# A four-layer network on one core: a band scratch with the heads innermost, a third thread for the last attention's maxima, and gates computed first

## The reference, cut to what matters

```
L0 attn  banded: 16 heads, each token looks at the 32 tokens up to itself;
         out = einsum('bntd,bntde->bnte', softmax(bond - 10 * damage), val_win)
L0 ffn   8 low-rank experts, gated per sequence
L1 attn  causal, 8 local heads over 512 tokens, 8 global heads over 128 compressed ones
L1 ffn   8 experts, 128 -> 512 -> 128, gate = softmax of the top 2
L2 attn  linear: q, k = relu(.) + eps; kv = k'v; z = 1 / (q . sum(k) + eps)
L2 ffn   16 experts of width 64, top 4 gates, and one shared expert
L3 attn  16 heads of width 8: softmax(q k' * scale) v, divided by
         denom = mean over batches and tokens of the norm of each head's output
L3 ffn   64 experts of width 64, sigmoid gates, best 4 of 8 groups, top 8, and one shared
```

## Time and profile before

| | us |
|---|---|
| median of three runs (lowest, highest) | 3850.13 (3846.57, 3855.36) |
| the profiled execution | 3852.74 |
| its span, first to last instruction | 3851.0 |
| mean granted TensorE clock | 0.878 of full speed |
| DMA traffic | 355.91 MB, 331910 packets, 98529 of them under 512 B |

### The profile page before, as it was taken

The page is one execution under the profiler, slowest core; times in us unless marked ns, Lnnn a source line. Parts: engine busy times, 40 slices in busy tenths (PEclk is TensorE's granted clock), DMA queues, the critical chain, the costliest instruction groups (busy, mean ns, idle before and its releaser), DMA issues.

```text
span 3851.0 us, 43741 instructions
## 1 busy us (share of the span) xinstructions
PE 3115.1 (81%) x16174; PEld 1567.3 (41%) x16174; DVE 2426.6 (63%) x4576; ACT 1662.7 (43%) x2458; POOL 596.6 (15%) x425
## 2 busy tenths in 40 slices
PE   3647868997699868997699968998699977996698
PEld 1124423553245433554245532554235532464145
DVE  4634876568756776568765776668755786634442
ACT  3504625465255634465154644446154643432231
POOL 2001000311023010321013010321013110211030
PEclk8568969998799979998699989998799988997696
DMA  3151175302842165402843047412753128412261
GB/s 112 27 95 58 46 123 139 113 14 77 145 144 68 28 106 154 124 22 60 152 133 88 20 104 121 151 39 50 136 133 102 32 81 136 137 58 65 57 203 45
DMA packets 331910, 355.91 MB, mean 92 GB/s; under 512 B 98529, under 2 KB 264225, under 8 KB 330081
## 3 DMA queue, kind: packets, MB, share of 16 engines
q1 hardware_dynamic: 331697, 353.11, 39.1%
HBM read 302.74 MB, written 49.66 MB: 92 GB/s over the span
## 4 chain that ended last, share of the span: by engine, by line
PE 52%; DVE 28%; DMA 7%; ACT 5%; issue 4%; POOL 2%; SPq 2%; ACTq 0%; DVEq 0%; POOLq 0%
DVE MX L1596 7%; PE PS L1805 6%; PE PS L1828 6%; PE PS L1832 5%; PE PS L1659 5%; PE PS L1667 5%; PE PS L1103 3%; DVE U L891 3%; PE PS L1773 3%; DVE U L898 3%; DMA UU<-k_scratch 3%; PE PS L1784 2%; DVE D L1650 2%; POOL D L1404 1%; DVE D L948 1%
## 5 line engine op out<-in xcount | busy, mean ns | idle before, releaser
L1404 POOL TENSOR_TENSOR D<-D,GW 128x512 f32<-128x512 f32 x320 | 434.7, 1359 | 1409.1 <-ACT D L1477 1173.6
L783 ACT ACTIVATE U<-U 128x2048 f32<-128x2048 f32 x256 | 488.0, 1909 | 184.3 <-DVE U L891 99.4
L1645 DVE SCALAR_TENSOR_TENSOR D<-D,PS 128x512 f32<-128x512 f32 x336 | 229.2, 682 | 399.2 <-ACT D L1481 283.6
L1477 ACT ACTIVATE D<-PS 128x512 f32<-128x512 f32 x336 | 200.2, 596 | 610.2 <-PE PS L1828 610.2
L1805 PEld LDWEIGHTS PS<-WST,D 128*128 128x128 f32 (+1 forms) x2688 | 353.0, 198 | 163.4 <-DVE D L1650 96.0
L1805 PE MATMUL PS<-WST,D 128*128 128x128 f32 (+1 forms) x2688 | 380.3, 286 | 29.3 <-DVE D L1650 29.2
L1832 PE MATMUL PS<-XT,WST 128*128 128x512 f32 (+1 forms) x672 | 372.6, 637 | 29.2 <-DVE D L1645 28.0
L898 DVE SCALAR_TENSOR_TENSOR U<-PP,RD,QB 128x512 f32<-128x512 f32 x512 | 364.1, 780 | 47.5 <-ACT QB L780 28.8
L1103 PE MATMUL PS<-U,resident 128*32 128x512 f32 x2048 | 304.6, 675 | 102.3 <-ACT U L783 102.3
L1828 PE MATMUL PS<-XT,WST 128*128 128x512 f32 (+1 forms) x672 | 369.6, 633 | 7.7 <-DMA WST<-in_pairs_dram 4.7
L1596 DVE TENSOR_REDUCE MX<-PS 128x2 f32<-128x1024 f32 x256 | 298.4, 1221 | 84.9 <-PE PS L1751 84.9
(11 more groups left out here) (345 smaller groups left out, 3907.2 us busy)
## 6 DMA issues: line engine op xcount, KB each, us to landing
GW<-gates_scratch SPq DMA_DIRECT2D x320, 256.0 KB, 4.3
WST<-in_pairs_dram SPq DMA_DIRECT2D x336, 192.0 KB, 2.4
U<-band_scratch SPq DMA_DIRECT2D x32, 1280.0 KB, 14.6
UU<-in_w_dram SPq DMA_DIRECT2D x64, 512.0 KB, 7.6
UU<-pad_scratch SPq DMA_DIRECT2D x8, 1792.0 KB
UU<-q_scratch SPq DMA_DIRECT2D x24, 384.0 KB
UU<-k_scratch SPq DMA_DIRECT2D x24, 384.0 KB
e_scratch<-D SPq DMA_DIRECT2D x8, 1024.0 KB, 4.5
```

Source lines behind the costliest of these rows:

```text
L783: e.activation(ring(i), ring(i), ACT.Gelu).then_inc(S["act"], 1)
L1404: e.tensor_tensor(AV[:, n % 3, :], AV[:, n % 3, :], GW[:, p // 2 % GWS, p % 2, :], ALU.mult).then_inc(S["gated"], 1)
```

## The change

1. **Band scratch.** Its shape becomes (4, 128, 160, 16): the head is the innermost index. A row's weights go out as one run of 32 x 16 numbers (2 KB) in place of 16 runs of 32 (128 B), and come back as one run of 160 x 16 numbers (10 KB) in place of 16 runs of 160 (640 B). TensorE's moving operand at L1154 (L1167 after) is then read with 64 bytes between its elements. Zeroing the scratch at the start has the same runs.
2. **Third thread c** (turn 1): the split of q and k, their way out and back, the scores and maxima and the way of the negated maxima into the stack. It is woven among the layer-3 pairs. The scores are now 64 steps of one matmul in PZ(2), each after the maximum of the one before; a maximum covers one bank, not two. s2 stands behind the pairs, with the two sums of the exponentials (`sel_den`) as steps of its own, 66 steps in all, and their reciprocals and the norm work behind it. The sum of squares of a sequence (`norm_sum`, `norm_copy`, `norm_store`) goes to the next sequence's f1, and for the last sequence to the end of its thread.
3. **Gates first.** Layer 2's gate matmul and top 4 come before the linear attention, layer 3's gates directly behind the gate matmul, and its pairs directly behind them.
4. **Buffers.** RC and N3 lie in the gate tiles; the expert weights of f1 lie in GW (experts 0 to 3) and UU (4 to 7), where they were all in UU; the first matmul of a sequence's f1 waits for the last exponential of the sequence before.
5. **Final loads.** `sp_before_final` stands behind the last pair loads (it stood before them), and loads six sequences in place of seven; the seventh is loaded behind s2's scores.

The core of the diff; a_ lines first, the table STARTS (and TURN = 428.30, now 415.20) left out:

```diff
-        z_dram = nc.dram_tensor("band_scratch", (NT, NH, P, BAND), FP32).ap()
+        z_dram = nc.dram_tensor("band_scratch", (NT, P, BAND, NH), FP32).ap()
-                dst = bass.AP(z_dram.tensor, j * NH * P * BAND, [[BAND + 1, P], [P * BAND, NH], [1, HOR]])
+                dst = bass.AP(z_dram.tensor, j * NH * P * BAND, [[(BAND + 1) * NH, P], [1, HOR * NH]])
-                e.dma_start(band(j), z_dram[j].rearrange("n p t -> p n t")).then_inc(S[f"band{j}"], 16)
+                e.dma_start(band(j), z_dram[j]).then_inc(S[f"band{j}"], 16)
-                                            band(j)[:, 8 * h + 2 * q + r, 0:w], start=(j == 0 and r == 0),
+                                            band(j)[:, 0:w, 8 * h + 2 * q + r], start=(j == 0 and r == 0),
...
+        RC = G4[:, :, :, :].rearrange("p (h k) j n -> p h (k j n)", h=2)
+        w1slot = lambda x: (GWF, UU)[x // 4][:, 2 * FF * (x % 4):...]
...
+        def c_dve(e, b):
+            e.wait_ge(S["qk3"], at("qk3", b, 2))
+            yield from dve_split(e, F3[:, :, :], lambda k: SPL3[:, :, k, :], "split3")
+            for k in range(64):
+                yield
+                e.wait_ge(S["s1_3"], at("s1_3", b, k + 1))
+                e.tensor_reduce(MX3[:, k % NT:k % NT + 1, k // NT], PSall[:, 6:7, :], AX.X, ALU.max)...
+        def c_pe(e, b):
+            for k in range(64):
+                yield
+                if k == 0:
+                    e.wait_ge(S["stacked3"], ...); e.wait_ge(S["padded3"], ...); e.wait_ge(S["qk3"], ...)
+                else:
+                    e.wait_ge(S["max3"], at("max3", b, k))
+                e.matmul(PZ(2), QS3[:, hd, P * j:P * j + P], KS3[:, hd, :], start=True, stop=True)...
...
             yield from b_pe_pairs(e, b, 3)        # b_pe: now before s2
+            for x, k in enumerate(B_STEPS):       # s2, 64 scores and two sums
+                if x == 0:
                     e.wait_ge(S["nm_in3"], at("nm_in3", b, 48))
+                    e.wait_ge(S["sl"], at("sl", b, 2 * PAIRS))
+                    e.wait_ge(S["uv"], at("uv", b, PAIRS))
+                    e.wait_ge(S["b_f"], at("b_f", b, 3))
+                if k is None:
+                    e.matmul(PZ(x % 3), cn("sel_den"), OS3[:, h, :], start=True, stop=True)...
...
                             if b > 0:             # b_pe, first matmul of f1
-                                e.wait_ge(S["b_f"], at("b_f", b - 1, 3))
+                                e.wait_ge(S["p3"], at("p3", b - 1, STEPS3))
...
+            if b == B - 1:                        # b_sp, behind the pair loads
+                sp_before_final(e)
+                if x == 4:
+                    e.wait_ge(S["s2_3"], at("s2_3", b, STEPS3 - 1))
+                    if b == B - 1:
+                        final_load(e, B - 2, "fin_in7")
...
-            weave(thread(a_sp, e, 0), thread(b_sp, e, 1))
+            weave(thread(a_sp, e, 0), thread(b_sp, e, 1), thread(c_sp, e, 1))
```

More of the change, by code:

```diff
@@ L1701, in b_pe @@
             w2 = cn("qkv2")
+            for j in range(NT):
+                last = e.matmul(PZ(0)[:, 2 * P + E2 * j:2 * P + E2 * j + E2], XT(b)[:, P * j:P * j + P], cn("gates")[:, 8:8 + E2], start=(j == 0), stop=False, skip_group_check=True)
+            last.then_inc(S["gate_ps"], 1)
             e.matmul(PZ(1), w2[:, 0:C], XT(b), start=True, stop=True).then_inc(S["l2_ps"], 1)
@@ L1717, in b_pe @@
             yield
+            e.wait_ge(S["gate_dve"], at("gate_dve", b, 3))
+            for j in range(NT):
+                last = e.transpose(PZ(0)[0:E2, P * j:P * j + P], GT[:, j, 0:E2], ident)
+            last.then_inc(S["gate_ps"], 1)
+            yield
             e.wait_ge(S["l2_dve"], at("l2_dve", b, 4))
@@ L1731, in b_pe @@
             w3 = cn("wqkv3")
+            for j in range(NT):
+                last = e.matmul(PZ(0)[:, E3 * j:E3 * j + E3], XT(b)[:, P * j:P * j + P], cn("gates")[:, 24:88], start=(j == 0), stop=(j == NT - 1), skip_group_check=True)
+            last.then_inc(S["gate_ps"], 1)
             for k in range(2):
@@ L1758, in b_pe @@
             last.then_inc(S["gate_ps"], 1)
-            yield
-            e.wait_ge(S["nm3"], at("nm3", b, 1))
-            for j in range(NT):
-                last = e.transpose(PZB(1)[0:48, P * j:P * j + P], NM3[:, j, :], identb[:, :])
-            last.then_inc(S["nm_t3"], 1)
+            yield from b_pe_pairs(e, b, 3)
             def weighted(s):
@@ L1860, in sp_before_final @@
                 e.wait_ge(S[s], at(s, B - 1, 0))
-            for k in range(B - 1):
+            for k in range(B - 2):
                 final_load(e, k, "fin_in")
@@ L1945, in _ @@
             ready(e)
-            weave(thread(a_act, e, 0), thread(b_act, e, 1))
+            weave(thread(a_act, e, 0), thread(b_act, e, 1), thread(c_act, e, 1))
             act_final(e)
@@ L1952, in _ @@
             ready(e)
-            weave(thread(a_dve, e, 0), thread(b_dve, e, 1))
+            weave(thread(a_dve, e, 0), thread(b_dve, e, 1), thread(c_dve, e, 1))
             dve_final(e)
@@ L1959, in _ @@
             ready(e)
-            weave(thread(a_pe, e, 0), thread(b_pe, e, 1))
+            weave(thread(a_pe, e, 0), thread(b_pe, e, 1), thread(c_pe, e, 1))
             pe_final(e)
```

375 lines of the change are left out of this document (202 added, 173 removed), and 180 rows, old and new, of tables (PER, STARTS).

## The result

| | before | after |
|---|---|---|
| median (lowest, highest), us | 3848.73 (3846.57, 3855.36) | 3914.84 (3911.44, 3916.76) |
| span of the profiled execution | 3851.0 | 3915.0 |

The ratio is 1.0168, 95% interval 1.015 to 1.0185: the change makes the kernel 1.7% slower, 66 us. I had forecast 3690 and a range up to 3790, with 0.13 on slower.

The account below looks back on a forecast made before the run. It took thread b's chain to set the round of 440.4 where TensorE was not full. Head 312, seven rounds of 427 (2989), last b 312 and final 77 gave 3690; own range 3635 to 3745, wider 3615 to 3790.

Parts of the forecast that it names:

- The head: Start of the kernel, thread a alone: shorter band transfers save 20, from 332.6 to 312.
- The stride: Band matmuls in a round: strided reads take 2.2 times as long, 1.22 to 2.7, so 6 more per round.
- 58 less of thread b's chain: Per round: 45 for maxima and their way into the stack, 8 of way out, 5 from layer 2's gates.
- What comes back: Per round, pairs' stage: 17 more for 64 score matmuls and 20 more for thread a's displaced TensorE work.
- counted from TensorE: Round's second sum: busy 370, idle 68.4 less 34.2 plus 13 of gate chain and 8 of weave, giving 425.
- The gates' chain: Ahead of layer 3's pairs: 21 of the way out's 29 stay in a round; 26 in the last b.
- The crowd: Rounds: the band's transfers stay hidden behind thread b's matmuls as before, so nothing more was counted.
- The weave: Pairs' stage: scores and maxima waiting among pair steps cost 8 a round, bounds 0 to 32, balanced by clock gain 8.
- The last b: Last sequence's thread b stretch: from 359 to 312, with 26 gate chain, 106 pairs, 44 s2 and 12 behind it.
- The 11.6 that one transfer ... held them up: Pairs of the last b: an 11.6 hold-up by one transfer under the final loads would be gone.
- B: Rival: strided quarters are read one after the other, 38 a round in place of 6, period 459, total 3922; chance 0.14.
- A: Rival: round hardly shortens, 438 to 442, through a costlier weave or strided reads sharing a port; total 3781; chance 0.22.

Follow-up runs that it names:

- only_band: The kernel before with nothing but the new band scratch layout: 3841.75, ratio 0.9956.
- seam_norm: Changed kernel with f1's first products ahead of its row of gates and the previous sequence's sum of squares at f1's fifth expert: 3894.57.
- before_cheap: The kernel before with last-attention scores and maxima over the first 32 of 512 keys only: 3794.63, ratio 0.9844.
- band_cheap: The kernel before with the new band layout and scores and maxima over 32 keys only: 3629.33, ratio 0.9416.
- light_stack: Changed kernel with only a quarter of q and k (128 of 512 tokens) loaded back into the stack: 3850.97, ratio 0.9999.
- band_old: Changed kernel with the band scratch laid out as before, heads outermost: 4054.85, ratio 1.0506.
- nogate_light: Changed kernel with layer 3's choice of experts left out and a quarter of the stack's q and k loads: 3837.86, ratio 0.9952.
- three_off: Changed kernel with seam_norm's edits, scores and maxima over 32 keys, and a quarter of the stack's loads together: 3783.36, ratio 0.9816.
- seam_fill: Changed kernel with f1's first products moved ahead of its row of gates on TensorE and ScalarE: 3917.21, ratio 1.0164.

## Why the prediction was wrong, step by step

**The head** held: 20 less forecast, 26 measured, which only_band shows to be the band layout by itself. The band's way from the last copy to the output's copy took 20.3 (181.5 to 201.8) where it had taken 40. The prediction's own parts for it add to 23 and not to "about 20". The other 6 stand ahead of the last copy already (181.5 for 187.4): 2.4 of them at the first layernorm step (34.4 for 36.8), behind the zeroing of the scratch, which the sum left out; the rest I did not trace.

**The stride** held in kind and was too large: 6 a round forecast, 4 by L1167's rows and 3.4 by only_band. It was no cause of the loss. Here the rule of the Trainium skill in "SBUF — State Buffer" (Door 1) fits no better than before: a stride of 16 elements costs 1.9 times and one of 4 elements 2.2 times, where the page has 4 as the end of what is free.

**"58 less of thread b's chain"** held as a length: from q, k, v to s2 or to the pairs, whichever came next, was 75 and is 24, 51 less, but layer 2 gave 1 in place of 5. **"What comes back"** held too: the pairs' stage grew by 35 where I had 37 in all.

**The step that failed** is the one that follows, "counted from TensorE ... idle 68.4 less the emptied stage's 34.2, plus 13 ... and 8". It let all other idle time stand as it was. By the windows TensorE idles 77.8 in a round now, not 55, and is busy 379, not 370. Of the 22.6 of idle time above the sum, f1 has 13.4 (14.2 for 0.8) and the pairs 5.6 (they grew by 13.6 where the weave had 8); the rest is small. The 9 of busy time are about the 8 that I had taken off for full clock. What was left out:

- The seam. I costed the new places of the norm work and of f1's start at nothing in a round. f1 took 85.9 from its first product to its last and takes 114.2. This is not all loss: its first product (2106.4) now stands 20 ahead of thread a's closing step, L576 at 2126.0, where it stood 20 behind it (2104.7 and L563 at 2084.6), and of the 29 that its windows grew by, 15.6 are other busy time of TensorE. 13.4 are idle, 10 of them in the first window; mending it locally brought 20 us in all (seam_norm).
- The gates' chain. "I set 21 of the 29 as staying" scaled up layer 2's 11.2, whose store of 32 KB takes 1.6 (median); the 8.6 of layer 3's store is not in it. From q, k, v to the first gating is 35.9 in the round and 36.0 in the last b (3619.17 to 3655.19), where I had 21 and 26. In the gates' window the idle time is the 13 forecast (14.4), and the rest shows behind it: 5.0 in which the first down of the pairs waits, and a low clock there.
- The crowd. "In the rounds the band's transfers are hidden behind thread b's matmuls now as before, so nothing more is counted" was wrong twice. Before, what hid them were the scores and maxima (before_cheap, band_cheap). After, the stack's loads hold up the gates' store (light_stack gains 64 us), and the band's loads the weights of the pairs: without the short band transfers the loss would be 5.1% (band_old).
- The weave. I took 8 of waits, and that was its size (63.1 / 8 for the maxima). The wait of down for L1700 grew by 6 more, but light_stack takes 4 of them away, so most of it belongs to the gates' store. I booked the weave as balanced by a clock gain of 8, and the clock in the pairs fell from 0.97 to 0.91 where it should have risen.

**The last b.** Its +26 is the pairs, 132 where I had 106:

```profile
3642.00:3774.00 132.00, 113.24 (x464) 63.90 (x463) 88.81 (x136) 36.39 (x67) 40.53 (x32) 0.92 0.54 156
```

Beside them s2 has 6 more than the sum and the rest together some 6 less; f1, 79.9 for 59.3, starts before thread a is through here too and ends no later behind it than before. TensorE idles 19 in the pairs. 9 of that lie in their first 38 us, at a clock of 0.78, where the first gating comes late, and the negated maxima of the last sequence, behind the final loads, hold up s2 for 5.8, which I had at 0 with bounds 0 to 10. "The 11.6 that one transfer ... held them up" was misread: TensorE waited 4.7 there. In the chain of waits one also sees the loop that the single bank can make:

```profile
3694.29 0.70 DVE D L1695
...
3695.01 0.69 DVE D L1700
3695.70 0.61 DVE MX L1670
...
3696.36 0.39 PE PS L1864
3696.75 0.87 PE PS L1906 x2
...
3697.64 0.70 DVE D L1695
```

A pair's two VectorE steps, a maximum, the next score and v follow one another, 3.35 a turn, with neither engine full. It holds for a few turns only; many others in that chain are TensorE's matmuls back to back, 3.1 a turn. The +7 of the final is the last sequence's norm work, which now ends behind 3831; from the load of norm_scratch on the final is as long as it was, 76.

**What stays open.** With the seam mended, cheap maxima and a light stack the new order takes 3783, and the old order with the same band and cheap maxima 3629. Of the 154, 49 are busy time of the 32-column scores, which take 94.5 in all among the pairs and 45.6 in a row. The choice of experts is worth 13 (18 by the ratios) in the one pair of runs that shows it, light_stack and nogate_light. The rest is in waits that the table of waits names (in three_off 102.4 for thread a's L1120 behind ScalarE and 53.9 for its L1128, with the start of the pairs beside them), but no run separates them.

**The rivals.** The time came out near B's 3922, but not by B's mechanism: the strided reads cost 4 a round, not 38. That nearness is chance. A had the weave and the nearly full pairs right in kind, but the pairs were 86% busy, not above 90%. No rival spoke of transfers that meet.

## What to carry to other kernels

A stage in which the bounding engine idles may be cover for something else: before it is emptied, ask what of the other thread lands in its time (here the band's way, for which TensorE waited 170 us in place of 31 once scores and maxima were cheap), and what chain it ran beside (here the gates). Moving such a stage moves its transfers too, and those must be added up, in MB, for the window in which they now meet, with the small store that the next stage hangs on. And a count of saved idle time has to go through every other window of the round: in seam_fill products ran earlier, and f1 ended as late as before. A long transfer in the chain of waits is not a stop of that length; the view of waits has the stop.

## What the runs showed of the hardware

- With 64 bytes between its elements, a moving operand of TensorE in fp32 took 1.9 times as long as a contiguous one (2.28 for 1.22, both at full clock), with four quarters of the array reading at once; with 16 bytes, alone, 2.2 times. These rows give no sign that the four streams hold one another up.
- Stores of 256 KB with runs of 2 KB landed in 2.1 us each (median; the line below is of one round of the changed kernel), where runs of 128 B had taken 17.4. The packets fell from 331910 to 201354.

```profile
band_scratch<-D SPq DMA_DIRECT2D x4, 256.0 KB, 2.1
```

- A store of 128 KB took 8.6 us behind the stack's 2.3 MB of loads (with 1 MB of e_scratch between them in a round, without it in the last b), 2.3 with a quarter of the stack's, and 12.9 when the gates were ready 6.7 us sooner behind q, k and v: the first gating behind it came no earlier (36.3 for 35.9).
